# Low parts of the probabilities for two slots at a time, in place, with the products four slots behind

## The reference

```python
q = _qdq(layernorm(x)) @ _qdq(wq).T + bq          # 8-bit fake quantisation
kv = ctx @ wkv.T + bkv;  k, v = split(kv)         # in full precision
attn = softmax(q k^T / sqrt(32))                  # (8, 16, 512, 1601)
o = attn @ v
x = x + _qdq(o) @ _qdq(wp).T + bp
x = x + experts(layernorm(x))                     # top 2 of 8 experts
```

## Time and profile before

| | us |
|---|---|
| median of three runs (2266.59 to 2273.07) | 2271.1 |
| the profiled execution | 2265.57 |
| its span, first to last instruction | 2263.9 |
| TensorE busy with products | 1835.3 |
| VectorE busy | 1737.2 |
| ScalarE busy | 1351.9 |
| GpSimd busy | 879.7 |

### The profile page before, as it was taken

One profiled execution on the slowest core, in us unless ns is written; L12 is line 12 of the kernel. 1 busy time (PEld: TensorE's weight loads), 2 busy tenths in 40 slices (PEclk: granted clock), 3 DMA queues, 4 the chain that ended last, 5 costly groups with the idle time before them and its releaser, 6 DMA issues. The chain is left out here.

```text
span 2263.9 us, 60188 instructions
## 1 busy us (share of the span) xinstructions
PE 1835.3 (81%) x24804; PEld 1264.4 (56%) x24804; DVE 1737.2 (77%) x2304; ACT 1351.9 (60%) x1944; POOL 879.7 (39%) x821
## 2 busy tenths in 40 slices
PE   1479999998989998998989999899962569999920
PEld 1257776666667666666766666677641135555500
DVE  4469999999889998999999899899974734443434
ACT  0357877777678777777877777787664413232300
POOL 0011552563364346336434733653252022221156
PEclk9889999999999999999999999999985589999965
DMA  2322322332333233223323322322202534444368
GB/s 84 103 79 50 107 75 61 91 102 74 72 98 91 61 90 103 72 78 89 98 59 86 107 76 77 89 80 57 64 29 97 169 103 145 145 142 149 126 202 267
DMA packets 151106, 223.23 MB, mean 99 GB/s; under 512 B 29744, under 2 KB 82992, under 8 KB 150832
## 3 DMA queue, kind: packets, MB, share of 16 engines
q1 hardware_dynamic: 135344, 175.28, 26.7%
q0 software_dynamic: 10880, 35.66, 5.5%
q10 hardware_dynamic: 4608, 8.39, 1.0%
HBM read 119.05 MB, written 60.83 MB: 79 GB/s over the span
## 5 line engine op out<-in xcount | busy, mean ns | idle before, releaser
L764 DVE TENSOR_TENSOR a_p_low<-a_p 128x1024 f16<-128x1024 f32 (+1 forms) x896 | 1095.4, 1245 | 135.7 <-ACT a_p L642 127.3
L642 ACT ACTIVATE a_p<-ps_s 128x1024 f32<-128x1024 f32 (+1 forms) x896 | 862.5, 967 | 382.8 <-PE ps_s L493 375.1
L493 PE MATMUL ps_s<-a_q_stack,a_k_stack 96*128 96x512 f16 (+1 forms) x1664 | 514.7, 384 | 80.7 <-DMA a_k_stack<-a_k_parts 58.2
L604 PE MATMUL ps_o<-a_v,a_p 128*128 128x65 f16 (+1 forms) x6656 | 447.6, 194 | 17.5 <-ACT a_o_sums L668 8.1
L604 PE MATMUL ps_o<-a_v,a_p_low 128*128 128x65 f16 (+1 forms) x6656 | 447.4, 194 | 0.0
L526 PEld LDWEIGHTS ps_p<-wkv,a_ctx 128*128 128x128 f16 x4992 | 330.3, 99 | 163.3 <-DVE a_v L779 56.4
L526 PE MATMUL ps_p<-wkv,a_ctx 128*128 128x128 f16 x4992 | 379.5, 222 | 42.0 <-DVE a_v L779 41.7
L604 PEld LDWEIGHTS ps_o<-a_v,a_p 128*128 128x128 bf16 (+1 forms) x6656 | 352.4, 98 | 98.3 <-DVE a_p_low L764 24.8
L510 PE MATMUL ps_p<-a_ctx,wkv 128*128 128x384 f16 (+2 forms) x1536 | 348.2, 337 | 37.3 <-DVE a_ctx L402 34.6
L604 PEld LDWEIGHTS ps_o<-a_v,a_p_low 128*128 128x128 f16 (+1 forms) x6656 | 317.9, 98 | 0.0
L510 PEld LDWEIGHTS ps_p<-a_ctx,wkv 128*128 128x128 f16 x1536 | 148.1, 98 | 185.0 <-DVE a_ctx L402 31.3
(11 more groups left out here) (219 smaller groups left out, 2041.0 us busy)
## 6 DMA issues: line engine op xcount, KB each, us to landing
a_k_stack<-a_k_parts SPq DMA_DIRECT2D x384, 80.0 KB, 2.1
d_ys<-f_y SPq DMA_DIRECT2D x72, 256.0 KB, 2.5
a_ctx_raw<-in_ctx_dram SPq DMA_DIRECT2D x64, 192.0 KB, 2.5
a_q_stack<-d_q_t SPq DMA_DIRECT2D x96, 128.0 KB, 3.5
a_xm<-in_x_dram SPq DMA_DIRECT2D x8, 1024.0 KB, 5.8
a_ctx_raw<-in_ctx_dram SPq DMA_DIRECT2D x32, 256.0 KB, 4.7
d_q_t<-a_q_parts SPq DMA_DIRECT2D x32, 256.0 KB, 2.7
d_q_full<-a_xm SPq DMA_DIRECT2D x32, 256.0 KB, 2.9
```

The costliest lines, as they stand in the source:

```text
L493: mm = pe.matmul(t["ps_s"][s % 2][0:r, n * N:(n + 1) * N], t["k_stack"][v % 2][0:TERMS * DH, j, kt * P:kt * P + r], t["q_stack"][v % 2][0: ...
L604: mm = pe.matmul(t["ps_o"][:, q * VC:(q + 1) * VC], part[0:r, n * N + q * P:n * N + (q + 1) * P], val, start=(g == 0 and n == 0 and low == ...
L642: act.activation(t["p"][s % NP][0:r, 0:len(tiles) * N], t["ps_s"][s % 2][0:r, 0:len(tiles) * N], ACT.Exp, scale=float(DH) ** -0.5 / WSCALE ...
L764: dve.tensor_tensor(t["p_low"][s % NP][0:r, 0:n], full, high, ALU.subtract).then_inc(lows, 1)
```

## The change

VectorE makes the low parts of two slots with one operation. A buffer of `a_p` now holds the probabilities of two neighbouring groups of one head (128x2048 f32), and there are three of them instead of four of 128x1024. Groups 0 and 1, 2 and 3, 4 and 5 make a pair; group 6 is alone, so a head has four pairs. In the first slot of a pair VectorE has no probability operation, and in the second it waits for the second exponential and works on both. Its output goes into the low 16 bits of each f32 word, as f16, beside the high part, and `a_p_low` is gone; TensorE reads the low parts with a step of two from the same buffer. `lows` counts pairs. ScalarE waits for `used` only ahead of the first slot of a pair, until the products of the pair three before are done. The products, and with them the copy of the sums, are four slots behind the scores instead of three.

```diff
--- before.py
+++ after.py
@@ -193,8 +193,9 @@
 SLOTS = HB * GROUPS
 UNITS = B * NBLK
 LAST = UNITS * SLOTS
-LAG = 3
-NP = 4
+LAG = 4
+NP = 3
+PAIRS = -(-GROUPS // 2)
 KEY_CUTS = [0, 512, 896, 1280, M]
 RANGE_TILES = [range(KEY_CUTS[r] // P, -(-KEY_CUTS[r + 1] // P)) for r in range(4)]
 STACK_CUTS = [0, KEY_CUTS[3], M]
@@ -211,6 +212,14 @@
 
 def group_tiles(g):
     return range(GROUP * g, min(GROUP * g + GROUP, KT))
+
+
+def pair_of(s):
+    return s // GROUPS * PAIRS + s % GROUPS // 2
+
+
+def first_slot(pair):
+    return pair // PAIRS * GROUPS + pair % PAIRS * 2
 
 
 def rows_of(kt):
@@ -590,19 +599,21 @@
             def do_values(s):
                 v, j, g = s // SLOTS, s % SLOTS // GROUPS, s % GROUPS
                 head = s // GROUPS
-                pe.wait_ge(lows, s + 1)
+                pair, at = pair_of(s), g % 2 * GROUP * N
+                pe.wait_ge(lows, pair + 1)
                 if g == 0 and head >= 1:
                     pe.wait_ge(out_copied, head)
-                p_high = t["p"][s % NP][:, :].bitcast(BF16).rearrange("p (n two) -> p n two", two=2)[:, :, 1]
+                p_high = t["p"][pair % NP][:, :].bitcast(BF16).rearrange("p (n two) -> p n two", two=2)[:, :, 1]
+                p_low = t["p"][pair % NP][:, :].bitcast(F16).rearrange("p (n two) -> p n two", two=2)[:, :, 0]
                 for n, kt in enumerate(group_tiles(g)):
                     r = rows_of(kt)
                     if j == 0 and kt * P in KEY_CUTS:
                         wait_freed(pe, ("v", v, KEY_CUTS.index(kt * P)))
                     val = t["v"][v % 2][0:r, kt, j, :]
-                    for low, part in enumerate((p_high, t["p_low"][s % NP])):
+                    for low, part in enumerate((p_high, p_low)):
                         for q in range(QT):
                             mm = pe.matmul(t["ps_o"][:, q * VC:(q + 1) * VC],
-                                           part[0:r, n * N + q * P:n * N + (q + 1) * P], val,
+                                           part[0:r, at + n * N + q * P:at + n * N + (q + 1) * P], val,
                                            start=(g == 0 and n == 0 and low == 0 and q == 0),
                                            stop=(kt == KT - 1 and low == 1), skip_group_check=True)
                 mm.then_inc(used, 1)
@@ -636,10 +647,11 @@
                 g = s % GROUPS
                 tiles = group_tiles(g)
                 r = rows_of(tiles[-1])
+                pair, at = pair_of(s), g % 2 * GROUP * N
                 act.wait_ge(scores, s + 1)
-                if s >= NP:
-                    act.wait_ge(used, s - NP + 1)
-                act.activation(t["p"][s % NP][0:r, 0:len(tiles) * N], t["ps_s"][s % 2][0:r, 0:len(tiles) * N],
+                if pair >= NP and g % 2 == 0:
+                    act.wait_ge(used, first_slot(pair - NP + 1))
+                act.activation(t["p"][pair % NP][0:r, at:at + len(tiles) * N], t["ps_s"][s % 2][0:r, 0:len(tiles) * N],
                                ACT.Exp, scale=float(DH) ** -0.5 / WSCALE).then_inc(shifted, 1)
 
             def keys_high(u, r):
@@ -756,12 +768,15 @@
 
             def low_probabilities(s):
                 g = s % GROUPS
-                tiles = group_tiles(g)
-                r, n = rows_of(tiles[-1]), len(tiles) * N
+                if g % 2 == 0 and g < GROUPS - 1:
+                    return
+                pair, tiles = pair_of(s), group_tiles(g)
+                r, n = rows_of(tiles[-1]), (g % 2 * GROUP + len(tiles)) * N
                 dve.wait_ge(shifted, s + 1)
-                full = t["p"][s % NP][0:r, 0:n]
+                full = t["p"][pair % NP][0:r, 0:n]
                 high = full.bitcast(BF16).rearrange("p (n two) -> p n two", two=2)[:, :, 1]
-                dve.tensor_tensor(t["p_low"][s % NP][0:r, 0:n], full, high, ALU.subtract).then_inc(lows, 1)
+                low = full.bitcast(F16).rearrange("p (n two) -> p n two", two=2)[:, :, 0]
+                dve.tensor_tensor(low, full, high, ALU.subtract).then_inc(lows, 1)
 
             def keys_low(u, r):
                 job = ("k", u, r)
@@ -967,8 +982,7 @@
         t["v"] = [sb(f"v{n}", [P, KT, HB, VC], F16) for n in range(2)]
         t["k_stack"] = [sb(f"k_stack{n}", [TERMS * DH, HB, M], F16) for n in range(2)]
         t["k_parts"] = sb("k_parts", [P, 2, M], F16)
-        t["p"] = [sb(f"p{n}", [P, GROUP * N]) for n in range(NP)]
-        t["p_low"] = [sb(f"p_low{n}", [P, GROUP * N], F16) for n in range(NP)]
+        t["p"] = [sb(f"p{n}", [P, 2 * GROUP * N]) for n in range(NP)]
         t["q_stack"] = [sb(f"q_stack{n}", [TERMS * DH, HB, N], F16) for n in range(2)]
         t["o_sums"] = [sb(f"o_sums{n}", [P, HB, QT, VC]) for n in range(2)]
         t["o_full"] = [sb(f"o_full{n}", [P, QT, C]) for n in range(2)]
```

## The result

The changed kernel takes 2333.1 us, median of 4 runs (2327.98 to 2337.5); the kernel before took 2272.1 in 4 runs beside them. The ratio is 1.026, 95% interval 1.022 to 1.030: the change costs 61 us. The prediction was 2247 (2214 to 2284), faster with a chance of 0.65. Time, sign and range were all wrong. The profiled execution took 2337.5 us, 4.4 above the median.

A forecast was written before the change was run, and what follows sets the result against it. The prediction took TensorE and VectorE, both 92% busy in the attention loop, to bound the kernel by waiting for each other in turn. Its terms, -17 - 6 - 1 + 0 = -24 us, gave 2247 us, range 2214 to 2284.

The forecast's parts named there:

- The operation itself: VectorE's low-part subtraction: a double operation takes about 2.33 us, with no saving of its own.
- the rival for it: The strided write on VectorE runs at half the rate, a pair takes 4.6 us, about +640 us, 2910; chance 2%.
- The mark that I had set: Sign of a wrong forecast: a double operation over 2.6 us on the mean without GpSimd beside it.
- TensorE's reads with a step of two: TensorE's loads of the low parts at that step cost nothing: 99 ns against 98 ns packed.
- Three buffers of two: Exponentials of g 0 and g 2 wait for products, 1.0 us later in unit 16; priced at nothing.
- my bound of +14: Upper bound in us for the wait for ScalarE's copy of the sums, 7.1 us before, left as it is.
- Slot 9: v0's low parts start earlier as the slot loses its operation; TensorE waits less at slot 11: -17 us.
- slot 16: v1's low parts start earlier in the same way; six units wait less at slot 18: -6 us.
- Slots 22 and 24: v2's low parts behind slot 22's double operation: new TensorE wait of 1.1 us; with slot 25, -1 us over 28 units.
- The late bank: Rival at slot 24: stacking transfers start 1.1 us later every unit, +31, half the gain remains: +19, 2290; chance 17%.
- GpSimd shut out: Rival: longer VectorE operations lock GpSimd out in seven units, +30 less 24: +6, 2277; chance 10%.
- Last unit and lag: Products of the last slot come one slot later, about 0.5 us, partly given back by the last unit's pairs: zero.

The follow-up runs named there:

- e5: Kernel before, packed low parts, each 128x1024 low-part operation on VectorE cut in three adjacent ones: 2359.8 us, ratio 1.038.
- e3: Kernel before, single slots, with only the low parts written in place into the low half of each word: 2332.0 us, ratio 1.025.
- the finer wait: Changed kernel, each half of a pair's buffer waiting only for the products that last read that half: 2324.6 us, ratio 1.022.
- the order: VectorE does low parts of keys and values ahead of the low probabilities: on the changed kernel 2317.2 us, on the kernel before 2233.6 us.
- e12: Kernel before with only LAG changed from 3 to 4, so products come four slots behind: 2404.7 us, ratio 1.056.
- both kernels with the finer wait: Changed kernel with ScalarE's wait split by buffer half, alone (2324.6 us) and with low parts of keys and values first on VectorE (2324.4 us).
- e2: Changed kernel with low parts written packed into the first half of the pair's buffer, output not the reference's: 2265.6 us, ratio 0.997.
- e1: Kernel before plus a phase ahead running the subtraction alone on VectorE: 1024 columns packed 1226 ns, strided 1293; 2048 strided 2424.
- e8: Kernel before plus a probe phase ahead, VectorE writes quiet and beside TensorE: at 1024 columns strided 1293 then 1403 ns, packed 1224 beside TensorE.

## Why the prediction was wrong

**The operation itself: the step that failed.** It took 2.33 us for a double operation, "no saving of its own", and said that no row of before shows such a write; the rival for it was all or nothing, half the rate at 2%. Measured: 2.29 packed (so 2.33 was right for a packed pair), 2.42 strided on a quiet core, 2.6 to 2.68 beside TensorE, 2.74 on the mean of the kernel. What was missing was the middle: 5 to 15% on an operation that makes up 70% of VectorE's work in the loop (902.9 of 1286.5 us from 200 to 1600 us in the trace of before). The mark that I had set, "over 2.6 us on the mean without GpSimd beside it", was reached (median 2.63). At the 0.59 and 0.73 us lost for each us more on VectorE in e5 and e3, a busy time 105 us above the packed kernel's gives 62 to 77, and 67.5 was measured. Of the 86 us between the forecast (2247) and the result (2333.1) these 67.5 are the strided write; the other 18.6 lie between the forecast and the packed kernel (2265.6), that is in the terms below.

**TensorE's reads with a step of two: right for TensorE.** The loads take 98 ns. But VectorE's half-word writes are slower beside TensorE's work (1403 for 1293); that the step of its reads plays a part was not tried. The Trainium skill (page "SBUF — State Buffer", section "🔬 SBUF: two separate sides") says that on the engine side only the port pair shared with GpSimd causes contention and that VectorE's own pair never waits. The packed writes agree; the strided ones do not, and the measurement decides.

**Three buffers of two: priced at nothing, wrong.** If the same 0.59 to 0.73 held for less work too, which no run shows, the packed kernel's 70 us less on VectorE would have given 41 to 51 us; it gave 7, so my estimate is that the structure costs some 35 to 45 us. With the strided write the finer wait brings back 8.5 and the order 16; e12 shows how dear such a wait becomes. That the exponential "still finds" its scores in time was argued from one slot of unit 16 with ScalarE at 76%; I never asked what a chain of such delays does to the copy of the sums (7.1 us to 22.4, above my bound of +14) and to the high parts behind it. How the 35 to 45 us divide between the wait, the pair's latency and the fourth slot is open, but for 8 us in the last unit (below): no run has packed pairs in a buffer of their own, and the finer wait was not tried with packed low parts in the pair's own buffer, whose first half holds the low parts of both slots and so does not come free after the first slot's products.

**Slot 9 right in kind, slot 16 not.** Counted slot by slot in units 1 to 30, TensorE's wait for the values at slot 11 went from 31.5 to 20.5 us (predicted -17). At slot 18 it went from 7.3 to 4.6 in front of the projection (-6), but 2.7 came in front of another job of that slot (L546), so that nothing was gained.

**Slots 22 and 24: the rival was real, through another door.** The wait at slot 24 came in 19 units, but at 0.8 us, 14.8 in all (2.9 in 7 units before); and a second one that I had not looked for, 16.6 us in 20 units at slot 22, for the low parts of the keys, whose operation of slot 19 stands behind a pair. The late bank was to cost by delaying the stacked keys; their wait shrank instead (53.2 to 28.2, or 58.6 to 37.8 with the unnamed one at slot 0), probably because TensorE had already lost the time at the banks.

**GpSimd shut out: happened, and is not needed for the loss.** Over the span it was busy 1106.9 us for 879.7. With packed pairs (e2) it is busy 936.7, with single strided operations (e3) 1046.6: most of the lengthening comes with the strided write, not with the longer operation on which I had put it. A kernel can lose as much without it: e5 has it at 785.2 and takes 27 us more than the changed kernel. But in both kernels with the finer wait TensorE waits at slot 0 for the stacked keys, 38.0 and 33.9 us, and in the wait looked at above it is GpSimd that holds them back. The Trainium skill (same page, section "Who interferes with whom") has a VectorE operation with two SBUF inputs and a GpSimd operation that reads SBUF shut each other out for the whole instruction. The trace agrees that GpSimd is lengthened; why a strided write lengthens it so much more than a packed one stays open.

**Last unit and lag.** Put at zero. From the first scores of unit 31 to the scores of its last slot the changed kernel takes 42.8 us and the packed one as well, for 36.3 before, and what follows is 1.8 us longer in both: 8.3 us, which is part of the structure's cost.

## What to carry to other kernels

Before a tensor is folded into the spare half of another, time the one operation that writes it, beside the engine that will read it: here a time 5 to 15% longer on an engine at 92% cost more than half the instructions were worth. When the wait table names two consumers of one engine, look at which has slack and put the other first in the list; that order, not the length, gave 40 us here. And do not price at nothing a wait for work that another engine issues at the end of the same step, when that engine in turn waits for what stands behind the waiting one: with every exponential waiting so, and the products one slot later, 127 us went.

## What was not expected of the hardware

VectorE writes 16-bit results into one half of each 32-bit word at 1293 ns for 1024 columns instead of 1226, into a quarter of 8 bytes at 2432, and f32 into every second word at 1226 (e1, e8). TensorE at work beside them slows the writes with a step of two, to 1403 ns, and leaves packed ones at 1224 (e8). An operation of one input pays too (736 for 694 ns, e8). A VectorE operation of 344 columns takes 575 ns in the loop of e5; three in a row overlap a little, and from 200 to 1600 us they are busy 1061.7 us in 646 slots, 1.64 us each, for 902.9 us in 688, or 1.31, with one of 1024 columns.
